# Delta-rule layers: v copied out by ScalarE, PSUM banks exchanged, output projection across the turn of a stage, VectorE's transpose and remainder later

## The chip, the cores and the metric

One core of a Trainium2 chip runs the whole program; its engines are TensorE, VectorE, ScalarE and GpSimd, and SyncE issues the DMAs. The metric is the device time of one execution in microseconds, here the median of three runs.

## The reference, cut to what matters

The program is a small audio tower: a convolutional token mixer, an attention and state-space layer, a mixture of experts, a fast-weight block and a second mixture of experts. The change touches the fast-weight block alone, which holds two delta-rule layers with a feed-forward part between them. One layer computes, for 16 sequences of 254 positions, 8 heads of 64:

```python
def step(W, inp):
    qt, kt, vt, bt = inp
    wk = jnp.einsum('bhde,bhe->bhd', W, kt)
    v_new = bt * (vt - wk)
    W = W + jnp.einsum('bhd,bhe->bhde', v_new, kt)
    out = jnp.einsum('bhde,bhe->bhd', W, qt)
    return (W, out)
...
h = layer_norm(x, ln_g, ln_b)
qkvb = jnp.einsum('sbi,oi->sbo', h, slow_w).reshape(slen, bsz, H, 3 * D + 1)
q, k, v, beta = jnp.split(qkvb, [D, 2 * D, 3 * D], axis=-1)
q = jax.nn.softmax(q, axis=-1)
k = jax.nn.softmax(k, axis=-1)
beta = jax.nn.sigmoid(beta)
attn = delta_rule(q, k, v, beta)
o = jnp.einsum('sbd,od->sbo', attn.reshape(slen, bsz, H * D), out_w)
return x + o
```

## The kernel before

`fast_weights` (L1487) handles one layer. A sequence of 254 positions is cut into two chunks of 127 (u = 0, 1). Within a chunk the recurrence is turned into a triangular system: A holds the products of keys with beta-scaled keys, its 32x32 diagonal blocks are inverted on VectorE, the blocks below the diagonal are joined by TensorE, and the system is solved against the right-hand side beta * v. The state goes from chunk 0 to chunk 1 through `next_state` and `carry`.

The layer is a software pipeline of 18 stages, written out by `stages` (L1590). In stage b each engine *prepares* batch b (projections, softmax, A, right-hand side, query-key products), *inverts* the diagonal blocks of batch b - 1, and *substitutes* (solves, outputs, output projection) batch b - 2. The first two stages and the last two do only some of this. Every engine has its own hand-written list of operations for a stage, and semaphores tie the lists together; nothing reorders them.

VectorE's list (from L2139): maximum and shift of the keys of both chunks, `turn_blocks` (L2107, the 32x32 transpose of the inverted blocks that came back by DMA), beta, sums and reciprocals, the queries' maxima and shifts, then the inversion of 31 steps, each a product (L2129) and a subtraction (L2133). Between its steps stand the queries' sums, `rest(0)` (L2098, the remainder for chunk 0, which needs TensorE's `join_rest`), the subtraction of the carried part (L2173), and `rest(1)`. After the inversion come the two right-hand sides (L2091), which read v in PSUM, `mask_qk(0)` (L2113), the addition of the output projection (L2184) and `mask_qk(1)`.

TensorE's list starts with the projections of keys, beta and queries (L1712), then `below_blocks` (L1768), the transposes of scaled keys and keys (L1723) with `corner_blocks` (L1784) between them, the first solve (L1800), `sum_a` (L1736), `join_rest` (L1813), the second solve (L1825), the v projection of chunk 0, `next_state`, `first_outputs`, `carry` (L1850), and so on; at the end stand `sum_qk(0)` (L1753), the output projection `project_out` (L1895) and `sum_qk(1)`, which waits for `rhs`, because v lies in the banks that it writes.

ScalarE takes the exponentials and copies results out of PSUM (L1954 transposes, L1961 A, L1968 the odd query-key products, L1975 solutions, L1981 corner blocks). GpSimd scales keys and queries (L1662, L1664, L1668), masks the odd query-key products (L1674) and resets `lane_x` (L1680). SyncE moves A and the inverse through DRAM.

The eight PSUM banks are shared by name. Keys are projected into banks 4 and 5, the same that `sum_qk(1)` fills and `mask_qk(1)` and `copy_qk(1)` read; queries go into 7 and 3, those of `sum_qk(0)`. So in the order above the keys' projection of the next stage waits for `mask_qk(1)`:

```python
PROJ_K, PROJ_Q, PROJ_V, BETA = (4, 5), (7, 3), (4, 5), 6
TURN_K, TURN_KB, TURN_Q = (4, 5), (6, 7), (3, 6)
SUM_A, SUM_QK = (4, 6), ((7, 3), (4, 5))
...
project("k", 0, PROJ_K[0], "qk_even", c)
project("k", 1, PROJ_K[1], "qk_copied", c)
```

## Time and profile before

| | us |
|---|---|
| median of 3 runs | 3041.76 (3034.02 to 3046.06) |
| the profiled execution | 3040.74 |
| its span, first to last instruction | 3039.0 |
| TensorE busy in the span | 2402.0 (79%) |
| VectorE busy | 2068.4 (68%) |
| ScalarE busy | 1234.0 (41%) |
| GpSimd busy | 747.4 (25%) |
| mean granted TensorE clock | 0.882 |

Busy shares are means over the whole program. The first delta-rule layer runs from about 1321 to 2006 us of the span, the second from about 2116 to 2810 us, the feed-forward part between them. In a timeline row stand start, duration, engine, line, operation, what it writes and reads, and in brackets the idle time before it with what ended that; PE is TensorE, DVE is VectorE, ACT is ScalarE, POOL is GpSimd. A TensorE row can hold many matmuls (x16). In a row of a stretch stand its ends and length, then the busy time (and instructions) of TensorE's matmuls and weight loads, VectorE, ScalarE and GpSimd, then the mean granted TensorE clock (1.00 is 2.4 GHz, 0.50 is 1.2 GHz), the DMA engines' share and GB/s. Matmuls are pipelined, so a busy TensorE is not one at its peak.

### The profile page before, as it was taken

What the parts mean: (1) busy time and instruction counts of PE and PEld (TensorE: products, weight loads), DVE (VectorE), ACT (ScalarE), POOL (GpSimd) and SP (SyncE); (2) the same over time, 40 slices, a digit from 0 to 9 for tenths busy, and PEclk for the clock granted to TensorE, in tenths of its full rate; (3) what the DMA queues carried; (4) which work ended last, traced back from release to release, by engine and by line L of the source; (5) the groups of instructions that cost most, each with busy time, mean ns of one, the idle gap of its engine ahead of it and who ended that gap; (6) DMA issues with size and microseconds to landing.
All of it is one profiled execution on the core that took longest, in us unless ns stands there. A gap on an engine that the chain in (4) does not pass through costs nothing. (4 is left out here: it accounts for less than half of the span.)

```text
span 3039.0 us, 44026 instructions
## 1 busy us (share of the span) xinstructions
PE 2402.0 (79%) x16426; PEld 1387.2 (46%) x16426; DVE 2068.4 (68%) x4427; ACT 1234.0 (41%) x1981; POOL 747.4 (25%) x712
## 2 busy tenths in 40 slices
PE   6747777778669999967888888687788888876598
PEld 2232222222234444335666666543466666665343
DVE  2256888888837777658888888613788888883332
ACT  3555555555432222343344443244334443431332
POOL 0005766676700000032222222101222222220000
PEclk9878998898879999988899999779789898986699
DMA  1000000000010000002222222100122222220000
GB/s 34 0 10 0 1 0 0 0 1 0 2 41 0 1 0 1 26 14 39 43 43 43 43 43 43 32 15 1 32 43 43 43 43 43 43 43 17 10 1 28
DMA packets 280818, 65.89 MB, mean 22 GB/s; under 512 B 272968, under 2 KB 274464, under 8 KB 280224
## 3 DMA queue, kind: packets, MB, share of 16 engines
q1 hardware_dynamic: 280608, 63.09, 11.2%
q8 instruction: 132, 2.16, 0.3%
q14 instruction: 78, 0.64, 0.1%
HBM read 44.20 MB, written 18.86 MB: 21 GB/s over the span
## 5 line engine op out<-in xcount | busy, mean ns | idle before, releaser
L949 POOL TENSOR_TENSOR ma_hc<-ma_state,ma_c 128x508 f32<-128x508 f32 x256 | 298.8, 1184 | 243.5 <-DVE ma_state L1048 144.3
L2133 DVE TENSOR_TENSOR fw_lane_x<-fw_lane_x,fw_lane_p 128x126 f32<-128x126 f32 (+22 forms) x992 | 326.8, 329 | 34.0
L2129 DVE TENSOR_TENSOR fw_lane_p<-fw_lane_a,fw_lane_x 128x126 f32<-128x126 f32 (+22 forms) x992 | 277.7, 280 | 29.6
L1712 PE MATMUL fw_p<-fw_w,fw_xs 128*127 128x512 f32 (+1 forms) x512 | 232.8, 589 | 54.0 <-DVE fw_qk L2113 26.3
L838 PE MATMUL ma_ps_y<-ma_hc,const 128*128 128x508 f32 x480 | 261.5, 672 | 16.4 <-POOL ma_hc L949 6.1
L1048 DVE TENSOR_TENSOR_SCAN ma_state<-ma_da,ma_ps_dbx 128x510 f32<-128x510 f32 x176 | 214.2, 1217 | 81.3 <-ACT ma_da L921 51.5
L1148 ACT ACTIVATE ex_sig<-ex_gate,ex_gate_scaled 128x508 f32<-128x508 f32 x128 | 87.6, 684 | 271.6 <-PE ex_gate L1118 271.6
L1674 POOL TENSOR_TENSOR fw_qk<-fw_qk,fw_masks 128x512 f32<-128x512 f32 x64 | 82.2, 1285 | 403.0 <-ACT fw_qk L1968 403.0
L838 PEld LDWEIGHTS ma_ps_y<-ma_hc,const 128*128 128x128 f32 x480 | 97.7, 213 | 154.3 <-issue 111.4
L1649 POOL MEMSET fw_k_rows<- 128x512 f32 x4 | 2.1, 525 | 659.1 <-POOLq L81 659.1
L1712 PEld LDWEIGHTS fw_p<-fw_w,fw_xs 128*127 128x127 f32 x512 | 91.4, 216 | 128.1 <-issue 118.8
L1975 ACT ACTIVATE fw_u_new<-fw_p 64x512 f32<-64x512 f32 x128 | 75.8, 592 | 159.5 <-PE fw_p L1825 107.6
L1109 PE MATMUL ex_total<-ex_weighted,ex_down 128*128 128x508 f32 x256 | 130.7, 592 | 10.8 <-DVE ex_weighted L1173 10.8
L1162 DVE SCALAR_TENSOR_TENSOR ex_gelu<-ex_gate,ex_bias,ex_sig 128x508 f32<-128x508 f32 x128 | 95.6, 747 | 64.0 <-ACT ex_sig L1148 64.0
L921 ACT ACTIVATE ma_da<-ma_dt,ma_a 128x508 f32<-128x508 f32 x176 | 124.2, 711 | 34.3 <-DVE ma_dt L995 34.2
L1668 POOL TENSOR_TENSOR fw_q_rows<-fw_q_rows,fw_total_q 127x512 f32<-127x512 f32 x64 | 66.8, 1043 | 285.9 <-DVE fw_total_q L2077 285.7
L1118 PE MATMUL ex_gate<-xn,ex_gate_up 128*128 128x508 f32 x256 | 131.7, 596 | 5.1 <-PEq L81 5.1
L1122 PE MATMUL ex_up<-xn,ex_gate_up 128*128 128x508 f32 x256 | 130.8, 593 | 0.0
L1753 PE MATMUL fw_p<-fw_q_t,fw_k_t 64*128 64x128 f32 x1024 | 75.7, 288 | 65.0 <-issue 65.0
L1042 DVE TENSOR_TENSOR ma_ps_dbx<-ma_ps_b,ma_dtx 128x508 f32<-128x508 f32 x176 | 118.5, 673 | 6.5 <-PE ma_ps_b L816 6.3
L1961 ACT ACTIVATE fw_a_t<-fw_p 128x1024 f32<-128x1024 f32 x64 | 65.6, 1024 | 114.3 <-PE fw_p L1813 95.2
L2302 DVE TENSOR_TENSOR ex_weighted<-ex_relu,ex_weight 128x508 f32<-128x508 f32 x64 | 43.8, 684 | 100.0 <-ACT ex_relu L2289 100.0
(310 smaller groups left out, 5149.4 us busy)
## 6 DMA issues: line engine op xcount, KB each, us to landing
fw_lane_a<-fw_a_dram SPq DMA_DIRECT2D x64, 256.0 KB, 4.2
fw_a_dram<-fw_a_t SPq DMA_DIRECT2D x128, 64.0 KB, 2.1
fw_x_dram<-fw_lane_x SPq DMA_DIRECT2D x64, 128.0 KB, 2.9
fw_x_rows<-fw_x_dram SPq DMA_DIRECT2D x128, 64.0 KB, 3.2
fw_x_t<-fw_x_dram SPq DMA_DIRECT2D x128, 64.0 KB, 2.7
x_in<-in_x SPq DMA_DIRECT2D x4, 512.0 KB
ex_gate_up<-in_gate_up SPq DMA_DIRECT2D x1, 2048.0 KB
out<-h SPq DMA_DIRECT2D x1, 2032.0 KB, 6.2
```

The lines of the kernel that those rows point to most:

```text
L838: pe.matmul(y_sum[h][:, 0:W2], k.ident, hc[(2 * n + h) % 8][:, :], start=n <= 1 and n - 1 in (-1, *PAIRED), stop=n == DS - 1)\
L921: act.activation(decay[:, :, 1:L + 1], two(dt[u][h][:, :]), ACT.Exp, scale=a[:, h, n:n + 1]).then_inc(s["da"], 1)
L949: pool.tensor_tensor(two(hc[m % 8][:, :]), state[m % 4][:, :, 1:L + 1], two(c_kept[n % 2][:, :]), ALU.mult).then_inc(s["hc"], 1)
L1042: dve.tensor_tensor(dbx[h][:, :, 1:L + 1], two(b_all[:, 0:W2]), two(dtx[u][h][:, :]), ALU.mult).then_inc(s["dbx"], 1)
L1048: dve.tensor_tensor_scan(line(state[m % 4][:, :, :]), line(decay), line(driven), 0.0, ALU.mult, ALU.add).then_inc(s["scan"], 1)
L1109: pe.matmul(total[:, 0:W2], down[:, e, j, :], weighted[n % 2][:, :], start=False, stop=n == NHF - 1).then_inc(s["downed"], 1)
L1118: pe.matmul(gate[j][:, 0:W2], gate_up[:, e, j * H:(j + 1) * H], x, start=True, stop=True).then_inc(s["gated"], 1)
L1122: pe.matmul(up[j][:, 0:W2], gate_up[:, e, I0 + j * H:I0 + (j + 1) * H], x, start=True, stop=True).then_inc(s["upped"], 1)
L1162: dve.scalar_tensor_tensor(gelu[j][:, :], gate[j][:, 0:W2], bias[:, e, j:j + 1], sig[j][:, :], ALU.add, ALU.mult).then_inc(s["gelu"], 1)
L1712: pe.matmul(bank[0:C, bk, u * NH:u * NH + n] if name == "beta" else bank[0:C, bk, 0:n], xs[:, u * C:(u + 1) * C], w[:, at:at + n], start=T ...
L2129: dve.tensor_tensor(p, lane_a[:, j:j + 1, j + 1:BLOCK].to_broadcast(shape), lane_x[:, 0:shape[1], j:j + 1].to_broadcast(shape), ALU.mult)\
L2133: dve.tensor_tensor(below, below, p, ALU.subtract).then_inc(inverted[j], 1)
```

## The change

- ScalarE copies v of each chunk from PSUM to a new tile `v_rows` (`copy_v`), the first behind `k_first`, the second behind `copy_a(1)`. The right-hand sides read this tile, and `sum_qk(1)` waits for the copy in place of `rhs`.
- Keys are projected and turned in banks 7 and 3, queries projected in 4 and 5. The keys' projection waits for `mask_qk(0)` and `copy_qk(0)` of the stage before, the queries' for `mask_qk(1)` and `copy_qk(1)`.
- `project_out` and the addition of its result are done a stage later: TensorE has them behind the queries' projections, VectorE behind the second `scale_kb`. A nineteenth stage holds only these two.
- On TensorE the first transpose of scaled keys stands ahead of `below_blocks`, and the second ones are exchanged.
- VectorE's `turn_blocks` moves from behind the keys' second shift to behind the queries' first, and `rest(0)` from behind step 8 of the inversion to behind step 10.

```diff
         q_rows = per("q_rows", [128, NH, D])
+        v_rows = per("v_rows", [C, NH, D])
...
-        PROJ_K, PROJ_Q, PROJ_V, BETA = (4, 5), (7, 3), (4, 5), 6
-        TURN_K, TURN_KB, TURN_Q = (4, 5), (6, 7), (3, 6)
+        PROJ_K, PROJ_Q, PROJ_V, BETA = (7, 3), (4, 5), (4, 5), 6
+        TURN_K, TURN_KB, TURN_Q = (7, 3), (6, 7), (3, 6)
...
                     if u == 0:
+                        pe.wait_ge(s["shift_q"], c + 2)
                         pe.wait_ge(s["k_t"], c + 2)
...
                         else:
-                            pe.wait_ge(s["rhs"], c + 2)
+                            pe.wait_ge(s["v"], c + 2)
...
                 def project_out():
-                    if not substitutes:
+
+                    if b < 3:
                         return
-                    pe.wait_ge(s["out_t"], upto[1])
+                    pe.wait_ge(s["out_t"], c - 4)
...
-                project("k", 0, PROJ_K[0], "qk_even", c)
-                project("k", 1, PROJ_K[1], "qk_copied", c)
+                project("k", 0, PROJ_K[0], "qk_even", max(c - 1, 0))
+                project("k", 1, PROJ_K[1], "qk_copied", max(c - 1, 0))
                 project("beta", 0, BETA, "q_t", c)
                 project("beta", 1, BETA, "q_t", c)
                 project("q", 0, PROJ_Q[0], "qk_even", c)
                 project("q", 1, PROJ_Q[1], "qk_copied", c)
+                project_out()
+                turn("kb", 0, kb[0], TURN_KB[0], "kb", "beta_exp", b + 1)
                 below_blocks()
-                turn("kb", 0, kb[0], TURN_KB[0], "kb", "beta_exp", b + 1)
                 turn("k", 0, k_rows[0], TURN_K[0], "rows_k", "shift_k", c + 1)
                 corner_blocks()
-                turn("kb", 1, kb[1], TURN_KB[1], "kb", "shift_q", c + 1)
                 turn("k", 1, k_rows[1], TURN_K[1], "rows_k", "shift_k", c + 2)
+                turn("kb", 1, kb[1], TURN_KB[1], "kb", "k_t", c + 1)
...
-                turn("q", 0, q_rows[0], TURN_Q[0], "rows_q", "shift_q", c + 2)
+                turn("q", 0, q_rows[0], TURN_Q[0], "rows_q", "k_t", c + 2)
...
                 sum_qk(0, 1)
-                project_out()
                 sum_qk(1, 0)
...
             stages(pe, stage)
+            stage(B + 2, 0, False, False, False)
...
+                def copy_v(u):
+                    if prepares:
+                        act.wait_ge(s["proj_v"], c + u + 1)
+                        act.wait_ge(s["rhs"], max(c + u - 1, 0))
+                        act.activation(v_rows[u][:, :, :], heads(bank[0:C, PROJ_V[u], :]), ACT.Copy)\
+                            .then_inc(s["v"], 1)
...
                     act.wait_ge(s["proj_beta"], c + 2)
+                    act.wait_ge(s["rhs"], c)
...
+                copy_v(0)
                 solved(1, 0)
                 copy_a(1)
+                copy_v(1)
                 turned("q", 0, TURN_Q[0], q_t[par][0])
...
-                        dve.wait_ge(s["proj_v"], c + u + 1)
+                        dve.wait_ge(s["v"], c + u + 1)
...
-                        dve.tensor_tensor(rhs[par][u][0:C], heads(bank[0:C, PROJ_V[u], :]), wide(beta[:, u]), ALU.mult)\
+                        dve.tensor_tensor(rhs[par][u][0:C], v_rows[u][:, :, :], wide(beta[:, u]), ALU.mult)\
...
+                def add_outputs():
+
+                    if b >= 3:
+                        r_at = k.r[:, cols(b - 3, L)]
+                        dve.wait_ge(s["projected"], b - 2)
+                        dve.tensor_tensor(r_at, bank[:, PROJECT, 0:L], r_at, ALU.add).then_inc(s["added"], 1)
...
                 shift("k", 1)
-                turn_blocks()
...
                 maximum("q", 0)
                 shift("q", 0)
+                turn_blocks()
                 sums("k", 1)
                 inverse_sums("k", 1)
                 scale_kb(1)
+                add_outputs()
                 maximum("q", 1)
                 shift("q", 1)
                 go_on(0, 6)
                 sums("q", 0)
                 inverse_sums("q", 0)
-                go_on(6, 8)
+                go_on(6, 10)
                 rest(0)
-                go_on(8, 12)
+                go_on(10, 12)
...
                 mask_qk(0)
-                if substitutes:
-                    r_at = k.r[:, cols(b - 2, L)]
-                    dve.wait_ge(s["projected"], batches)
-                    dve.tensor_tensor(r_at, bank[:, PROJECT, 0:L], r_at, ALU.add).then_inc(s["added"], 1)
                 mask_qk(1)

             stages(dve, stage)
+            stage(B + 2, 0, False, False, False)
```

## Rows read from the trace of the kernel before

**Rows 1.** Busy time by stretch: steady part of the first delta-rule layer.

```profile
1379.00:1892.00 513.00, 425.28 (x5409) 326.20 (x5408) 433.07 (x1183) 208.37 (x351) 126.56 (x129) 0.90 0.25 41
```

**Rows 2.** Waits of VectorE in that stretch: us in total, times, longest us.

```profile
DVE fw_top_k L2056 <- PE fw_p L1712: 20.8, 16, 2.2
DVE fw_rhs L2098 <- PE fw_p L1813: 12.2, 10, 2.1
```

**Rows 3.** Timeline of VectorE (start us, us, ..., [idle before]): first and last steady stage.

```profile
1379.08 0.69 DVE L2056 TENSOR_REDUCE fw_top_k<-fw_p 127x8 f32<-127x512 f32 x1 [2.23 <-PE fw_p L1712]
...
1892.31 0.69 DVE L2056 TENSOR_REDUCE fw_top_k<-fw_p 127x8 f32<-127x512 f32 x1 [1.28 <-PE fw_p L1712]
```

**Rows 4.** Timeline of VectorE in the reference stage.

```profile
1695.61 0.69 DVE L2056 TENSOR_REDUCE fw_top_k<-fw_p 127x8 f32<-127x512 f32 x1 [1.28 <-PE fw_p L1712]
...
1699.07 0.71 DVE L2107 STREAM_TRANSPOSE fw_x_turned<-fw_x_rows 128x512 f32<-128x512 f32 x1 [0.71 <-DMA fw_x_rows<-fw_x_dram]
...
1704.61 0.93 DVE L2129 TENSOR_TENSOR fw_lane_p<-fw_lane_a,fw_lane_x 128x31 f32<-128x31 f32 x1
...
1711.81 0.69 DVE L2098 TENSOR_TENSOR fw_rhs<-fw_rhs,fw_p 64x512 f32<-64x512 f32 x1 [0.82 <-PE fw_p L1813]
1712.53 0.28 DVE L2129 TENSOR_TENSOR fw_lane_p<-fw_lane_a,fw_lane_x 128x115 f32<-128x115 f32 x1
...
1717.81 0.69 DVE L2173 TENSOR_TENSOR fw_rhs<-fw_rhs,fw_p 128x512 f32<-128x512 f32 x1
...
1728.68 0.19 DVE L2129 TENSOR_TENSOR fw_lane_p<-fw_lane_a,fw_lane_x 128x16 f32<-128x16 f32 x1
1728.91 1.14 DVE L2133 TENSOR_TENSOR fw_lane_x<-fw_lane_x,fw_lane_p 128x16 f32<-128x16 f32 x1
1730.08 1.29 DVE L2091 TENSOR_TENSOR fw_rhs<-fw_p,fw_beta 127x512 f32<-127x512 f32 x2
1731.29 0.68 DVE L2113 TENSOR_TENSOR fw_qk<-fw_p,fw_masks 128x512 f32<-128x512 f32 x1
...
1732.67 0.69 DVE L2113 TENSOR_TENSOR fw_qk<-fw_p,fw_masks 128x512 f32<-128x512 f32 x1 [0.37 <-PE fw_p L1753]
1734.64 0.69 DVE L2056 TENSOR_REDUCE fw_top_k<-fw_p 127x8 f32<-127x512 f32 x1 [1.28 <-PE fw_p L1712]
```

**Rows 5.** Timeline of GpSimd in the reference stage.

```profile
1704.44 1.04 POOL L1664 TENSOR_TENSOR fw_k_rows<-fw_k_rows,fw_total_k 127x512 f32<-127x512 f32 x1
...
1728.69 1.32 POOL L1674 TENSOR_TENSOR fw_qk<-fw_qk,fw_masks 128x512 f32<-128x512 f32 x1 [9.72 <-ACT fw_qk L1968]
1733.34 1.27 POOL L1674 TENSOR_TENSOR fw_qk<-fw_qk,fw_masks 128x512 f32<-128x512 f32 x1 [3.34 <-ACT fw_qk L1968]
```

**Rows 6.** Timeline of TensorE in the reference stage.

```profile
1694.48 4.11 PE L1712 MATMUL fw_p<-fw_w,fw_xs 128*127 128x512 f32 x12 [0.88 <-DVE fw_qk L2113]
...
1716.23 1.11 PE L1850 MATMUL fw_p<-fw_state,fw_kb_t 64*128 64x64 f32 x16
...
1727.89 1.99 PE L1895 MATMUL fw_p<-fw_out_t,fw_w_out 128*128 128x254 f32 x8
1731.47 1.16 PE L1753 MATMUL fw_p<-fw_q_t,fw_k_t 64*128 64x128 f32 x16 [1.59 <-issue]
```

**Rows 7.** Timeline of ScalarE in the reference stage.

```profile
1724.86 0.59 ACT L1975 ACTIVATE fw_u_new<-fw_p 64x512 f32<-64x512 f32 x1 [1.33 <-PE fw_p L1825]
...
1728.01 0.60 ACT L1968 ACTIVATE fw_qk<-fw_p 128x512 f32<-128x512 f32 x1
```

**Rows 8.** A turn at the low clock: timelines, then two stretches.

```profile
1578.51 0.69 DVE L2056 TENSOR_REDUCE fw_top_k<-fw_p 127x8 f32<-127x512 f32 x1 [2.23 <-PE fw_p L1712]
...
1576.43 6.21 PE L1712 MATMUL fw_p<-fw_w,fw_xs 128*127 128x512 f32 x10 [0.88 <-DVE fw_qk L2113]
...
1576.43:1582.64 6.21, 6.21 (x11) 3.17 (x12) 3.77 (x7) 1.44 (x3) 1.66 (x2) 0.52 0.98 160
...
1578.51:1616.32 37.81, 31.70 (x417) 23.48 (x417) 33.32 (x91) 15.90 (x27) 9.29 (x10) 0.95 0.25 38
```

More of the change, by code:

```diff
@@ L1579, in fast_weights @@
             "exp_k", "exp_q", "total_k", "total_q", "recip_k", "recip_q", "rows_k", "rows_q",
-            "beta_exp", "beta_one", "beta", "kb", "rhs", "k_first", "turn_k", "turn_q", "turn_kb", "k_t", "q_t",
+            "beta_exp", "beta_one", "beta", "kb", "v", "rhs", "k_first", "turn_k", "turn_q", "turn_kb", "k_t", "q_t",
             "kb_t", "a_sum", "a_t", "qk_sum", "qk_even", "qk_copied", "qk_odd",
```

## The prediction

> **What bounds the kernel now.** Start with the busy times by stretch. In the steady part of the first delta-rule layer VectorE is busy 433 of 513 us and TensorE 425 [rows 1]. TensorE's figure also counts small matmuls that wait on others; VectorE's order of work is what the waits speak of. The waits of VectorE in that stretch are the second view: 20.8 us ahead of the keys' maximum (L2056) for TensorE's projection and 12.2 us ahead of the remainder (L2098) for TensorE's join [rows 2]. The third is VectorE's timeline. Thirteen stages take 1892.31 - 1379.08 = 513.2 us, 39.5 us each [rows 3]. Each layer has 14 stages that do all three parts (batches 2 to 15), so 28 in all; the second layer runs the same code and I count its stages alike.
>
> As reference I take one stage, from the keys' maximum at 1695.61 to the next at 1734.64: T = 1695.61, length 39.03 us [rows 4]. VectorE waits there 0.71 us (transpose L2107, for a DMA), 0.82 us (remainder), 0.37 us (second mask) and 1.28 us (the next keys). It also loses time that no wait shows: the last operation of the inversion takes 1.14 us, though the one before it, of the same 128x16 elements, takes 0.19 us [rows 4]; GpSimd's mask runs from 1728.69 to 1730.01 [rows 5]. The first product of the inversion takes 0.93 us in the same way, while GpSimd scales k_rows from 1704.44 to 1705.48 [rows 4, 5]. So a VectorE operation with both inputs in SBUF stands still while GpSimd works, and ends about 0.05 us behind it.
>
> **The change part by part,** on the reference stage.
>
> *Up to the subtraction of the carried part (L2173),* now at T + 22.20. Moving the transpose behind the first queries' shift takes away its 0.71 us wait: it would start some 5.1 us after T, while the data landed 3.46 us after T. GpSimd's second scaling then starts 0.71 us earlier, but the added output (L2184, 0.41 us) now stands ahead of the inversion, so the first product is held some 0.4 us less. VectorE would come to the remainder at T + 16.20 - 0.71 - 0.82 - 0.41 + 0.41 + 1.24 = T + 15.91, where 1.24 us are the two inversion steps that now precede it, each of two operations of 0.28 us (the row at 1712.53) with 0.03 us behind them [rows 4]. TensorE delivered its part just before T + 16.20 in this stage, so the two meet within a few tenths, and I take no wait. From the remainder's end to the end of the carry, TensorE and ScalarE need 1717.34 - 1712.50 = 4.84 us [rows 4, 6]; nothing in that chain is touched. So the carry ends at T + 15.91 + 0.69 + 4.84 = T + 21.44, and the subtraction starts at about T + 21.48. VectorE itself would be there at 22.20 - 0.71 - 0.82 - 0.41 + 0.41 = T + 20.67 and waits 0.8 us: this is what comes late next, and the 1.24 us put ahead of the remainder pay for it. **Gain 0.72 us.** Bounds: nothing, if TensorE comes later to the remainder; 1.5 us, if the subtraction need not wait.
>
> *From there to the end of the inversion* nothing moves: 12.24 us, the hold of 0.95 us (1.14 - 0.19) in it.
>
> *The right-hand side* (L2091, two operations, 1.29 us) reads v from SBUF instead of PSUM. ScalarE's two copies have the shape of its 0.60 us copy at 1728.01; they lie in its idle time, 1.33 us ahead of 1724.86 for one [rows 7]. Without that cover they would cost 0.6 us each. The price lies elsewhere: both inputs of L2091 are now in SBUF. And the wait of the second query-key products for `rhs` is gone, so they need not start at 1731.47; their other wait, for the queries' copy, is over when ScalarE goes on to the next copy at 1728.01 [rows 6, 7]. From there: 0.1 + 1.16 us of products, 0.6 us of copy, so GpSimd's second mask is ready at about 1729.97, where its first ends (1730.01) and the right-hand side begins (1730.08). Now it runs at 1733.34, beside work that reads PSUM [rows 5]. One of the three operations there would be held for the mask's 1.27 us, less the 0.15 us by which a held one overlaps its tail: **cost 1.1 us.** Bounds: 0, if both operations go ahead of the mask, and 1.3, the mask's whole length. I take 1.1, the value nearest the two held rows, in both of which GpSimd got in between VectorE's operations. The Trainium skill (SBUF — State Buffer, Who interferes with whom) says that whichever of the two starts first holds the shared ports for its whole instruction and the other blocks fully. The held rows agree with it. By that rule the order of arrival at 1730 us decides, and with VectorE's pair first the sum would be lower by this term.
>
> *The turn.* Now the first mask ends at 1731.97, and then come the added output, the 0.37 us wait, the second mask and 1.28 us for the projection: 2.67 us to the next keys. With the banks exchanged the projection needs only the first mask: 1.28 us after it, with the second mask (0.69 us) inside. **Gain 1.39 us.**
>
> *TensorE's clock at the turn.* Where TensorE runs at 1.2 GHz there, the wait for the keys is 2.23 us instead of 1.28; the six projections take 6.21 us instead of 4.11, at a mean granted clock of 0.52 [rows 6, 8]. The wait is longer than 1.6 us at 10 of the 28 turns into such stages now (one of them is shown), and what precedes it is little work on TensorE. Now its idle time there is 1.59 us, 1.16 us of products, then 0.88 us [rows 6]. After the change the output projection (1.99 us) is gone from this place, the products end at about 1729.3, and the projection starts at 1731.97 + 1.1 + 0.12 = 1733.2: one idle stretch of 3.9 us. So I take the low clock at nearly all turns: **cost 0.8 us** of the 0.95, because some falls will come behind the first projection. Bounds 0 and 0.95. What the low clock delays behind the turn I leave out: the stage that follows the low turn shown took 37.81 us at a mean clock of 0.95, shorter than the reference [rows 8].
>
> *Covered or neutral.* The output projection now lies between the query projections and the transposes, where TensorE waits anyhow for the turned blocks (at full clock it ends at 1698.59 + 1.99, which is T + 4.97, and they come at T + 5.1 + 0.71 [rows 4, 6]); without that cover it costs up to 1.99 us. The new waits of ScalarE's beta and of the k transposes are for things done a few us before. In the filling stages the copy adds 0.7 us ahead of the right-hand side and the exchanged banks save as much; in the draining ones the same projection and addition stand in a nineteenth stage, behind the same wait for `out_t`. All these I cost at 0, within 2 us a layer.
>
> **Sum.** 39.03 - 0.72 + 1.1 - 1.39 + 0.8 = 38.8 us a stage, against the mean of 39.5: 28 x 0.7 = 20 us. The profiled execution took 3040.74 us (span 3039.0), which gives 3021; the median of the runs shown is 1.0 higher, so I predict **3022 us**.
>
> **The rivals.**
> *The right-hand side goes first.* Both of its operations follow without a gap, GpSimd waits for them, and the masks read PSUM and pass. Then the 1.1 us fall away: 37.7 us a stage, 28 x 1.8 = 50 us, 2991. For it: the two sit back to back (1.29 us for two of 0.69). Against it: GpSimd entered between inversion operations every time it is seen.
> *The gain comes back as a later wait.* With transpose, output projection and turned blocks all later on TensorE, the join could come 1.5 us after VectorE's arrival, and the subtraction with it; then what is saved early is waited for at L2098 and L2173: 39.5 us a stage, 3042. For it: 12.2 us of such waits stand already [rows 2], and the transpose moves back by about 1.7 us from T. Against it: the remainder itself moves back by 1.24 us, which leaves TensorE almost as much time as it loses.
> *Slower: the low clock lasts through the output projection.* It falls in the idle stretch, the six projections take 2.1 us more, and the output projection, now ahead of the transposes, at the same ratio 3.0 us or more instead of 1.99. The blocks below the diagonal then start about 4 us after their place now (T + 8.4 instead of T + 4.3), the join comes 2 us after VectorE, and a stage takes 38.97 + 2.0 = 41.0 us, 1.5 more than now. From half of the stages on, this eats the gain; in three of four it gives 28 x (0.75 x 1.5 - 0.25 x 0.6) = +27 us, 3068. For it: the longer idle stretch, and the six projections of rows 8, all at the low clock. Against it: the stage behind them, at 0.95.
>
> **How the numbers follow.** Chances: forecast 0.50, right-hand side first 0.22, gain waited for later 0.14, slower 0.14. The forecast's own range, from its bounds, is 3006 to 3036. A measurement here can tell about 0.5%, 15 us: faster means below 3027, slower above 3057. Of the forecast some 0.35 lies below 3027 and 0.15 within; with the first rival faster is 0.57, same 0.29, slower 0.14. The range 2983 to 3050 takes in most of the first rival and all of the second, and leaves out the greater part of the slower case and the end of the first.
>
> **What would show it.** In the new profile: no wait ahead of L2107's transpose; a wait of about 0.8 us ahead of the carried subtraction; one of the right-hand side's operations, or the last inversion one, at 1.7 to 1.8 us (or 1.3) next to GpSimd's second mask; the granted clock near half over the projections; the wait ahead of the keys' maximum between 1.3 and 2.3 us less the second mask's 0.6. It is wrong if the right-hand side takes 0.69 us each with the mask behind it, or if the wait ahead of the remainder grows past 1.5 us.

## The result, and the profile after

The kernel after takes 3051.01 us (median of 20 runs, 3040.29 to 3066.80), the kernel before 3041.41 us in the same series (20 runs, 3033.35 to 3048.66). The ratio is 1.0034, with a 95% interval of 1.0022 to 1.0046: slower, by 10 us or 0.3%, and outside the range of the prediction, just above its upper end of 3050. The profiled execution took 3051.16 us (span 3049.3), so that the trace speaks for the median.

The thirteen stages of the first layer come first, as a row of a stretch, then VectorE's waits in them (us in total, times, longest us).

```profile
1380.10:1898.40 518.30, 419.79 (x5401) 314.64 (x5401) 442.52 (x1182) 217.89 (x377) 132.55 (x131) 0.91 0.25 42
```

```profile
DVE fw_top_k L2070 <- PE fw_p L1713: 23.4, 25, 1.6
DVE fw_rhs L2195 <- PE fw_p L1852: 19.1, 13, 2.5
DVE fw_rhs L2112 <- PE fw_p L1815: 0.4, 2, 0.2
```

A stage takes 518.3 / 13 = 39.9 us, 0.4 more than before [rows 1, 3]. The wait ahead of the remainder, 12.2 us before [rows 2], has shrunk to 0.4 (it is L2112 now), as was meant. In its place stand 19.1 us ahead of the subtraction of the carried part (L2195), where the waits of before show one of 1.2 us:

```profile
DVE fw_rhs L2173 <- PE fw_p L1850: 1.2, 1, 1.2
```

The wait for the keys (L2070) has not shrunk: 23.4 us for 20.8.

VectorE's timeline shows where in a stage that is. The first two rows belong to one stage, T = 1699.02, the others to the next, T = 1739.73, up to the keys of the one behind it.

```profile
1715.24 0.69 DVE L2112 TENSOR_TENSOR fw_rhs<-fw_rhs,fw_p 64x512 f32<-64x512 f32 x1
...
1722.42 0.69 DVE L2195 TENSOR_TENSOR fw_rhs<-fw_rhs,fw_p 128x512 f32<-128x512 f32 x1 [2.45 <-PE fw_p L1852]
...
1739.73 0.69 DVE L2070 TENSOR_REDUCE fw_top_k<-fw_p 127x8 f32<-127x512 f32 x1 [1.41 <-PE fw_p L1713]
...
1741.44 0.69 DVE L2070 TENSOR_REDUCE fw_top_k<-fw_p 127x8 f32<-127x512 f32 x1 [0.29 <-PE fw_p L1713]
...
1745.28 0.70 DVE L2121 STREAM_TRANSPOSE fw_x_turned<-fw_x_rows 128x512 f32<-128x512 f32 x1
...
1748.62 0.60 DVE L2150 TENSOR_TENSOR fw_lane_p<-fw_lane_a,fw_lane_x 128x31 f32<-128x31 f32 x1
...
1755.94 0.69 DVE L2112 TENSOR_TENSOR fw_rhs<-fw_rhs,fw_p 64x512 f32<-64x512 f32 x1
...
1761.53 0.69 DVE L2195 TENSOR_TENSOR fw_rhs<-fw_rhs,fw_p 128x512 f32<-128x512 f32 x1 [0.85 <-PE fw_p L1852]
...
1772.62 1.23 DVE L2154 TENSOR_TENSOR fw_lane_x<-fw_lane_x,fw_lane_p 128x16 f32<-128x16 f32 x1
1773.77 2.35 DVE L2105 TENSOR_TENSOR fw_rhs<-fw_v_rows,fw_beta 127x512 f32<-127x512 f32 x2
1776.15 1.29 DVE L2127 TENSOR_TENSOR fw_qk<-fw_p,fw_masks 128x512 f32<-128x512 f32 x2
1779.07 0.69 DVE L2070 TENSOR_REDUCE fw_top_k<-fw_p 127x8 f32<-127x512 f32 x1 [1.63 <-PE fw_p L1713]
```

Against the reference stage [rows 4] the transpose no longer waits, and the first product of the inversion takes 0.60 us for 0.93. The right-hand sides take 2.35 us for 1.29; beside them stands GpSimd's row, where the masks of both chunks follow each other (before, 3.3 us apart [rows 5]):

```profile
1772.54 3.03 POOL L1675 TENSOR_TENSOR fw_qk<-fw_qk,fw_masks 128x512 f32<-128x512 f32 x2 [9.52 <-ACT fw_qk L1979]
```

The new wait of 0.85 or 2.45 us is explained on TensorE: the second solve behind the remainder in the reference stage of before, then, in the same two stages of after, that solve, the carry, and the turn.

```profile
1712.64 1.12 PE L1825 MATMUL fw_p<-fw_rhs,fw_x_t 128*64 128x64 f32 x16 [0.87 <-DVE fw_rhs L2098]
```

```profile
1716.08 1.12 PE L1827 MATMUL fw_p<-fw_rhs,fw_x_t 128*64 128x64 f32 x16 [2.48 <-DVE fw_rhs L2112]
...
1721.26 1.11 PE L1852 MATMUL fw_p<-fw_state,fw_kb_t 64*128 64x64 f32 x16
...
1756.78 1.12 PE L1827 MATMUL fw_p<-fw_rhs,fw_x_t 128*64 128x64 f32 x16 [2.48 <-DVE fw_rhs L2112]
...
1760.37 1.11 PE L1852 MATMUL fw_p<-fw_state,fw_kb_t 64*128 64x64 f32 x16
...
1776.99 6.83 PE L1713 MATMUL fw_p<-fw_w,fw_xs 128*127 128x512 f32 x12 [3.83 <-DVE fw_qk L2127]
```

TensorE stands 2.48 us in both stages, waiting for VectorE's remainder, where in the reference stage it stood 0.87 us ahead of the same solve. The wait has changed sides. From the start of that solve to the end of the carry TensorE then needs 6.29 us in one stage and 4.70 in the other. The granted clock of the stretches from the remainder to the subtraction tells them apart (the third stretch is the turn ahead of T = 1739.73; columns as in [rows 1]):

```profile
1715.20:1722.40 7.20, 6.33 (x67) 4.80 (x67) 4.47 (x12) 1.57 (x3) 1.04 (x1) 0.76 0.01 3
1755.90:1761.50 5.60, 4.72 (x67) 3.69 (x67) 4.47 (x12) 1.57 (x3) 1.04 (x1) 1.00 0.01 3
1736.70:1741.40 4.70, 3.53 (x6) 1.51 (x6) 2.98 (x5) 0.22 (x1) 0.61 (x1) 0.65 1.12 195
```

The timelines and clocks of all 26 steady stages, 13 in each layer, fall into three kinds. In 10 TensorE stands 2.48 us, goes at 1.2 GHz for part of this chain (granted clock 0.76), and VectorE waits 2.45 us. In 8 it stands the same 2.48 us, goes at 2.4 GHz (1.00), and VectorE waits 0.85. In the other 8 the clock is low further up, from T + 3 to the join (0.84 or 0.85); TensorE then stands only 0.88 or 1.20 us, the chain goes at 1.00, and VectorE waits 0.85. The order of the kinds is the same in both layers. (Two of the expectations below say 9 for the first kind; it is 10, five in each layer.) At every turn between these stages the clock is low (0.50 to 0.57 over the projections), behind an idle stretch of 3.83 us.

Why TensorE now stands so long is seen ahead of the join. One group of transposes and the stretch from T + 3 to the end of the join, first in the reference stage of before, then in the stage T = 1739.73 of after:

```profile
1706.07 1.11 PE L1723 MATMUL fw_p<-const,fw_kb 128*128 128x128 f32 x4
...
1698.61:1711.76 13.15, 10.63 (x192) 9.21 (x192) 11.09 (x31) 6.41 (x11) 5.13 (x5) 0.74 0.08 13
```

```profile
1750.33 0.66 PE L1724 MATMUL fw_p<-const,fw_kb 128*128 128x128 f32 x4
...
1742.73:1754.30 11.57, 10.64 (x203) 8.54 (x201) 10.78 (x32) 6.28 (x11) 5.13 (x5) 1.00 0.07 11
```

In the reference stage the clock was low in part of this stretch, and the join ended at T + 16.15. In the stage of after the whole stretch goes at 2.4 GHz and the join ends at T + 14.57, though the output projection now stands ahead of it. In the kernel before 21 of the 26 stages have 0.63 to 0.72 from T + 3 on; in the kernel after 18 have 1.00. So TensorE comes earlier to the remainder, while VectorE comes to it later (T + 16.16 on the means, for T + 15.38).

The means over these 26 stages, from T, put the two kernels side by side (us; from the timelines of both traces):

| | before | after |
|---|---|---|
| start of the remainder (wait before it) | 16.34 (0.96) | 16.22 (0.06) |
| start of the carried subtraction (wait before it) | 22.44 (0.12) | 22.42 (1.47) |
| end of the inversion | 34.71 | 34.74 |
| end of the right-hand sides | 36.03 | 37.01 |
| end of VectorE's first mask | 36.62 | 37.73 |
| next keys | 39.54 | 39.87 |

### The profile page after: what moved, and what is told of

It reads as the page before. It is cut to its first block and busy times, and to the rows that moved or that the text cites. A ratio compares the mean times of both kernels' runs of the same rounds, so it can differ in the third digit from the quotient of the medians.

```text
span 3049.3 us, 44218 instructions
## 1 busy us (share of the span) xinstructions
PE 2393.6 (78%) x16426; PEld 1368.2 (45%) x16426; DVE 2089.8 (69%) x4427; ACT 1258.6 (41%) x2045; POOL 757.9 (25%) x712
## 5 line engine op out<-in xcount | busy, mean ns | idle before, releaser
L1713 PE MATMUL fw_p<-fw_w,fw_xs 128*127 128x512 f32 (+1 forms) x512 | 275.0, 679 | 147.3 <-DVE fw_qk L2127 119.7
L2150 DVE TENSOR_TENSOR fw_lane_p<-fw_lane_a,fw_lane_x 128x126 f32<-128x126 f32 (+22 forms) x992 | 267.5, 270 | 29.6
L1713 PEld LDWEIGHTS fw_p<-fw_w,fw_xs 128*127 128x127 f32 x512 | 106.2, 247 | 244.7 <-issue 235.0
L1675 POOL TENSOR_TENSOR fw_qk<-fw_qk,fw_masks 128x512 f32<-128x512 f32 x64 | 93.2, 1458 | 286.0 <-ACT fw_qk L1979 284.2
L1949 ACT ACTIVATE fw_k_rows<-fw_k_rows 127x512 f32<-127x512 f32 x64 | 40.3, 630 | 247.6 <-DVE fw_k_rows L2079 247.6
L1827 PE MATMUL fw_p<-fw_rhs,fw_x_t 128*64 128x64 f32 x1024 | 78.0, 234 | 61.1 <-DVE fw_rhs L2112 61.1
L1663 POOL TENSOR_TENSOR fw_kb<-fw_k_rows,fw_kb_scale 127x512 f32<-127x512 f32 x64 | 66.8, 1043 | 188.6 <-DVE fw_kb_scale L2097 188.6
```

Of the source, the lines that this page charges most:

```text
L1713: pe.matmul(bank[0:C, bk, u * NH:u * NH + n] if name == "beta" else bank[0:C, bk, 0:n], xs[:, u * C:(u + 1) * C], w[:, at:at + n], start=T ...
L2150: dve.tensor_tensor(p, lane_a[:, j:j + 1, j + 1:BLOCK].to_broadcast(shape), lane_x[:, 0:shape[1], j:j + 1].to_broadcast(shape), ALU.mult)\
```

## The experiments

The theory: a remainder that comes late leaves TensorE idle, its clock falls in the idle stretches there and at the turn, and GpSimd's mask holds the right-hand side. The main rival: the chain from the remainder to the subtraction is late at full clock too, or it is the new order at the turn that costs. Sixteen kernels were run beside the one of the change; "ratio" is against the kernel before, with its 95% interval. The exchange of the banks, the output projection's new place and the later transpose were not run each by itself; what is said of them is read from rows.

**The remainder back behind step 8** (kernel after, nothing else):

```diff
-                go_on(6, 10)
+                go_on(6, 8)
                 rest(0)
-                go_on(10, 12)
+                go_on(8, 12)
```

> The changed kernel with the remainder back behind step 8 of the inversion. Theory (the late remainder leaves TensorE idle ahead of its second solve, its clock falls in 9 of 26 stages, and the carry is late): the remainder starts near T + 15.0 instead of T + 16.2, the wait ahead of the carried subtraction shrinks from 0.85 or 2.45 us to below 0.5 us in all stages, the subtraction starts at T + 20.7 to 21.0 instead of 22.4 on the mean, a stage takes 38.2 to 38.7 us instead of 39.87, the time is about 3012 us. Rival (TensorE's own chain sets the carry, wherever the remainder stands): the subtraction stays at T + 21.8 or later, 3045 to 3055 us.

Measured: 3033.83 us, ratio 0.9967 (0.9949 to 0.9985). The wait ahead of the carried subtraction is 0.03 us in every stage, as the theory has it. But the stages alternate between 38.35 and 40.15 us, because in every second one the remainder is waited for, 1.8 us (waits of VectorE, from 1380 to 1893 us):

```profile
DVE fw_top_k L2070 <- PE fw_p L1713: 24.2, 25, 1.6
DVE fw_rhs L2112 <- PE fw_p L1815: 11.6, 7, 1.8
```

So 17 us come back by undoing this move alone, less than half of the 39 expected; the rest goes to a fall of the clock ahead of the join, which the theory had not priced (granted clock 0.82 from T + 3 on in the slower stages, 1.00 in the others).

**The converse: the late remainder alone, in the kernel before**

```diff
-                go_on(6, 8)
+                go_on(6, 10)
                 rest(0)
-                go_on(8, 12)
+                go_on(10, 12)
```

> The kernel before with one part of the change alone: the remainder of chunk 0 stands behind step 10 of the inversion in place of step 8. Nothing is left out. Theory (TensorE's clock falls in the stretch between its join and the carry because it waits there for a late remainder, wherever the rest of the work stands): VectorE comes to the remainder 15.38 + 1.24 = 16.6 us behind the keys' maximum, TensorE delivered at 16.34 on the mean, so the wait there goes from 0.96 to 0.1 us or less; the carry is ready 5.57 us behind the remainder's start, at 22.2, and VectorE waits about 0.8 us for it at full clock; in a quarter to a half of the stages it waits 2.4 us with a granted clock of 0.5 between join and carry. Stage 39.6 to 40.0 us, time 3043 to 3055. Rival (the falls there come from the other order at the turn and the output projection's new place): a wait of 0.8 us ahead of the carried subtraction in every stage and no fall there, stage 39.2 to 39.3, time 3032 to 3037.

Measured: 3047.24 us, ratio 1.0027 (1.0009 to 1.0045). The stage has 39.68 us; the remainder's wait is gone (0.04), and 0.85 us ahead of the carried subtraction stand in 22 of 26 stages, 2.4 to 3.4 in four:

```profile
DVE fw_rhs L2173 <- PE fw_p L1850: 19.2, 13, 3.4
```

The move pays for its own gain at full clock and loses where the clock falls. The time lies where the theory put it, but the low clock comes in fewer stages (4 of 26) than the quarter to half that it named.

**Idle stretches filled.** Matmuls of 512 columns, whose result nobody reads, keep TensorE busy; they add work and leave nothing out. In the kernel after, first at the turn, then between the join and the second solve of chunk 0, then in both places:

```diff
                 join_rest(0)
+                if substitutes and prepares:
+                    for n in range(2):
+                        pe.matmul(bank[:, OUT, 0:512], k.ident, w[:, 0:512], start=True, stop=True)
...
                 sum_qk(1, 1)
+                if substitutes and prepares:
+                    pe.wait_ge(s["out_t"], upto[1])
+                    for n in range(3):
+                        pe.matmul(bank[:, OUT, 0:512], k.ident, w[:, 0:512], start=True, stop=True)
```

> The changed kernel with three extra 128x512 matmuls behind the second query-key products, into a bank that is rewritten before anyone reads it; they do no work of the reference. Theory (the idle stretch of 3.9 us on TensorE brings its clock to 1.2 GHz for the next projections, which costs the keys' maximum 0.7 to 0.9 us): the granted clock stays at 1.0 over the turn, the wait ahead of the keys' maximum falls from 1.4 to 1.63 us to about 0.7 us, about 3027 us. Rival (the extra matmuls stand ahead of the projection and delay it, or the clock falls anyway): the wait stays or grows, 3051 us or more.

Measured: 3025.64 us, ratio 0.9938 (0.9913 to 0.9962). The keys are waited for 0.68 us in every stage behind a filled turn, and the wait ahead of the second keys' maximum is gone. The waits ahead of the carried subtraction remain (1.44 us on the mean).

> The changed kernel with two extra 128x512 matmuls between TensorE's join and its second solve, into a bank that is rewritten before anyone reads it; they do no work of the reference. Theory (the wait for the late remainder lets TensorE's clock fall, which makes the carry late in 9 of 26 stages): no stage has the clock at 0.5 from T + 18.6 on, the wait ahead of the carried subtraction is about 0.85 us in all stages, 28 x 0.5 us less, about 3036 us. Rival (the clock falls for another reason, or the chain is as long at full clock): waits of 2.45 us remain, 3048 to 3055 us.

Measured: 3043.17 us, ratio 1.0000 (0.9983 to 1.0016). Between the remainder and the subtraction the clock is 1.00 in all 26 stages, as the theory has it. But the time expected was 3036, and half of the gain is missing: 18 stages wait 0.85 us for the carry, 8 wait 1.5 to 1.85, and in these the clock is low ahead of the join (0.81 to 0.85), so that the extra matmuls stand in the way of the solve. The stage takes 39.61 us. Part of the falls only moved.

> The kernel after with two matmuls of 512 columns between the join and the second solve of chunk 0 and three behind the last query-key products; their result is not used, nothing is left out. Theory (what the step up to the carried subtraction missed is TensorE's clock alone): the wait for the keys is 0.68 us, that ahead of the second keys' maximum is gone, the wait ahead of the carried subtraction is 0.85 in every stage: 39.34 - 0.73 - 0.29 = 38.3 us a stage, time 3051 - 28 x (39.87 - 38.3) = 3007, bounds 3000 to 3015. Rival (the clock falls in another stretch then, or the chain from remainder to carry is late at full clock too): 38.7 us or more a stage, 3018 to 3030, as with the fill at the turn alone.

Measured: 3005.60 us, ratio 0.9870 (0.9839 to 0.9902), and 38.31 us a stage. The stretch of thirteen stages and its waits:

```profile
1377.70:1874.30 496.60, 448.11 (x5531) 320.59 (x5531) 441.53 (x1182) 216.76 (x377) 132.68 (x131) 0.99 0.25 43
```

```profile
DVE fw_rhs L2202 <- PE fw_p L1852: 13.1, 13, 1.5
DVE fw_top_k L2077 <- PE fw_p L1713: 10.1, 14, 1.6
```

At a mean granted clock of 0.99 the subtraction starts at T + 21.41 or T + 21.42 in most stages (predicted: 21.48) and the kernel is 45 us faster than after, although TensorE does more. The theory's number was 3007. In 7 stages of the 26 VectorE waits 1.5 us and in one 1.85, where the theory had 0.85 in every one. The rival, a chain that is late at full clock too, falls: at full clock the wait is 0.85, near the 0.8 of the prediction.

**GpSimd's masks made to wait.** A wait in GpSimd's loop keeps its mask behind the right-hand sides, first for the second mask alone:

```diff
                 for u in chunks:
+                    if u == 1:
+                        pool.wait_ge(s["rhs"], c + 2)
                     pool.wait_ge(s["qk_copied"], c + u + 1)
```

> The changed kernel with one wait more: GpSimd's second query-key mask waits until both right-hand sides are done. Theory (the right-hand side is held by that mask because both its inputs lie in SBUF): the two right-hand sides take 1.3 us instead of 2.35, the next keys come about 1.0 us earlier, 28 x 1.0 us less, about 3023 us. Rival (the right-hand side is slower by itself, from its source or its broadcast factor): it stays near 2.3 us and the time at 3051 us or above.

Measured: 3003.96 us, ratio 0.9873 (0.9845 to 0.9901). The right-hand sides take 1.28 us again (VectorE's timeline; the operation ahead of them is still held, by the first mask):

```profile
1714.56 1.23 DVE L2156 TENSOR_TENSOR fw_lane_x<-fw_lane_x,fw_lane_p 128x16 f32<-128x16 f32 x1
1715.71 1.28 DVE L2107 TENSOR_TENSOR fw_rhs<-fw_v_rows,fw_beta 127x512 f32<-127x512 f32 x2
```

This shows the hold; the rival, a right-hand side that is slower by itself, falls. The gain is 1.6 us a stage and not the 1.0 expected, because the turn's idle stretch on TensorE shrinks too, from 3.83 to 2.76 us: the keys are then waited for 0.68 us in 19 of 26 stages.

**VectorE's first mask ahead of the right-hand sides**, so that the keys' projection starts earlier (kernel after):

```diff
+                mask_qk(0)
                 right_hand_side(0)
                 right_hand_side(1)
-                mask_qk(0)
                 mask_qk(1)
```

> The changed kernel with VectorE's first query-key mask ahead of the two right-hand sides. Theory (of the turn's 5.1 us from the end of the inversion to the next keys, the hold by GpSimd's mask and the projection's wait are the cost, and the mask of 0.7 us is all that the projection needs): the first mask runs beside GpSimd's, a right-hand side is held about 0.5 us instead of 1.07, the projection runs beside the right-hand sides at full clock and the keys' maximum waits for nothing; 3.0 to 3.2 us from the inversion's end to the next keys, a stage of 37.9 us or less, 2990 us or less. Rival (the clock at the turn falls for the idle time that is left, and the right-hand sides are held in full): a stage of 39 us, 3025 to 3051.

Measured: 3000.47 us, ratio 0.9867 (0.9834 to 0.9899); from the end of the inversion to the next keys 3.0 us, as expected. The time was expected at 2990 or less and missed that by 10 us: the clock now falls at the start of the stage (0.65 to 0.75 from T + 3 on in 20 of 26 stages), and waits ahead of the remainder (0.60 us on the mean) and the subtraction (1.17) stay. With the remainder back behind step 8 as well:

> Both the first mask ahead of the right-hand sides and the remainder behind step 8. Theory: the gains add, a stage of 37.0 us or less in most stages, 2975 us or less. Rival (TensorE's clock falls ahead of the join instead and the remainder waits 1.8 us in every second stage, as it did with the earlier remainder alone): no better than with the mask first alone.

Measured: 3005.03 us, ratio 0.9868 (0.9836 to 0.9901). The wait moved from the subtraction to the remainder, 1.77 us on the mean: the rival. Where the clock falls ahead of the join, the remainder's place was worth nothing here.

**The copy of v.** The kernel after without the copies:

```diff
-                            pe.wait_ge(s["v"], c + 2)
+                            pe.wait_ge(s["rhs"], c + 2)
...
-                copy_v(0)
...
-                copy_v(1)
...
-                        dve.wait_ge(s["v"], c + u + 1)
+                        dve.wait_ge(s["proj_v"], c + u + 1)
...
-                        dve.tensor_tensor(rhs[par][u][0:C], v_rows[u][:, :, :], wide(beta[:, u]), ALU.mult)\
+                        dve.tensor_tensor(rhs[par][u][0:C], heads(bank[0:C, PROJ_V[u], :]), wide(beta[:, u]), ALU.mult)\
```

> The changed kernel without the copy of v: the right-hand sides read PSUM again and the second query-key products wait for them; banks, output projection, transpose and remainder stay as changed. Theory (with the banks exchanged the copy brings no wait to an end that matters, and its price is the hold): the right-hand sides take 1.3 us, the second products fill TensorE's idle stretch, the next keys come 3.7 to 4.2 us after the inversion instead of 5.1, a stage of 38.6 us or so, about 3015 us. Rival (the copy is needed, for the second products now delay the projection of the next keys and the mask behind it): 5 us or more from the inversion to the next keys, 3045 us or more.

Measured: 3044.85 us, ratio 1.0005 (0.9990 to 1.0020). The right-hand sides take 1.29 us, but VectorE's second mask then waits 0.7 to 1.62 us for its products, and from the end of the inversion to the next keys it is some 4.8 us, for 5.1 in the kernel after. The expectation of 3015 missed and the time is the rival's: the copy's hold costs about what the copy saves elsewhere. The comparison is not clean, since the clock falls in the chain in 15 stages here and in 10 in the kernel after. The kernel before with the copies alone (the same lines the other way round, with `copy_v` as in the change; banks, order and output projection as before):

> The kernel before with another part alone: v is copied out by ScalarE, the right-hand sides read the copy, and the second query-key products wait for the copy in place of the right-hand sides; banks, order and output projection stay as before. Nothing is left out. Theory (two operands in SBUF let GpSimd's second mask in between, as in the kernel after): the pair of right-hand sides takes 2.3 to 2.4 us in place of 1.29, the wait ahead of VectorE's second mask (0.37 us) is gone, the wait for the next keys stays 1.3 to 2.2 us, since they are still projected behind that mask. From the end of the inversion to the next keys 5.3 to 5.6 us in place of 4.8, time 3055 to 3065. Rival (the second products, copied and masked earlier, give back what the hold takes): 4.8 us or less, time 3035 to 3045.

Measured: 3039.74 us, ratio 1.0001 (0.9971 to 1.0030). The expectation missed, the hold does not come. Rows of VectorE, GpSimd and TensorE at the end of one stage:

```profile
1731.25 1.28 DVE L2101 TENSOR_TENSOR fw_rhs<-fw_v_rows,fw_beta 127x512 f32<-127x512 f32 x2
...
1732.97 1.27 POOL L1675 TENSOR_TENSOR fw_qk<-fw_qk,fw_masks 128x512 f32<-128x512 f32 x1 [1.69 <-ACT fw_qk L1976]
...
1729.18 1.98 PE L1896 MATMUL fw_p<-fw_out_t,fw_w_out 128*128 128x254 f32 x8
1731.09 1.16 PE L1754 MATMUL fw_p<-fw_q_t,fw_k_t 64*128 64x128 f32 x16
```

Here the output projection still stands ahead of the second products, GpSimd's mask becomes ready only at 1732.97, and the right-hand sides, with the same two operands in SBUF, run through. So the copy alone does not bring the hold; by these rows it also takes second products that are ready earlier, with the output projection out of their way. No run moved the projection alone. The Trainium skill (SBUF — State Buffer, Who interferes with whom) says that the order of issue, not the form of the operation, decides who blocks. The 1.28 us here and 2.35 us in the kernel after, for the same statement, agree with it.

**Put together.** Remainder behind step 8 and the second mask waiting:

> The changed kernel with GpSimd's second mask behind the right-hand sides and the remainder back behind step 8. Theory (the two losses are of different places, so their gains add: 1.6 us a stage from the mask's wait, 0.6 us from the earlier remainder, as measured one by one): 37.6 us a stage, 2986 us. Rival (both gains come from the same falls of TensorE's clock, which go elsewhere): no better than the mask's wait alone, 3004 us.

Measured: 2975.02 us, ratio 0.9774 (0.9747 to 0.9801), 37.22 us a stage. Expected were 2986. The two gain more than their sum: the remainder is waited for 0.35 us on the mean, where it was 0.89 with the early remainder alone, and the subtraction 0.09, where it was 1.64 with the mask alone. That each shortens a stretch in which the clock fell for the other fits these waits but is not shown. Then both masks waiting:

```diff
                 for u in chunks:
-                    if u == 1:
-                        pool.wait_ge(s["rhs"], c + 2)
+                    pool.wait_ge(s["rhs"], c + 2)
                     pool.wait_ge(s["qk_copied"], c + u + 1)
```

> The kernel after with the remainder back behind step 8 of the inversion and both of GpSimd's masks (not the second alone) waiting for the second right-hand side. Nothing is left out. Theory (the last operation of the inversion, 1.14 us where the one before it takes 0.19, is held by the first mask in the same way): it takes 0.2 us, the right-hand sides stay at 1.2 us for the pair, the stage loses another 0.9 us against the version in which the second mask alone waits: 2975 - 28 x 0.9 = 2950, bounds 2945 to 2960. Rival (the hold moves to the next operation with both operands in SBUF, or the wait for the next keys takes it up, since it is TensorE's projection behind the first mask that ends last): 2970 to 2980.

Measured: **2932.84 us, ratio 0.9640** (0.9617 to 0.9663), 35.64 us a stage. VectorE's timeline and GpSimd's:

```profile
1729.52 0.19 DVE L2155 TENSOR_TENSOR fw_lane_x<-fw_lane_x,fw_lane_p 128x16 f32<-128x16 f32 x1
1729.62 1.28 DVE L2106 TENSOR_TENSOR fw_rhs<-fw_v_rows,fw_beta 127x512 f32<-127x512 f32 x2
...
1730.99 2.49 POOL L1676 TENSOR_TENSOR fw_qk<-fw_qk,fw_masks 128x512 f32<-128x512 f32 x2 [11.41 <-DVE fw_rhs L2106]
```

The last operation of the inversion takes 0.19 us for 1.23, and no operation is held in its place. The gain was expected at 25 us and is 42: beside the 0.96 us that the operation loses, the mean granted clock of the thirteen stages is 0.98 where it was 0.95 (0.91 in the kernel after). The same wait in the kernel before:

> The kernel before with one change alone: both of GpSimd's masks wait for the second right-hand side. Nothing is left out. Theory (only the hold of the last inversion operation goes, since the right-hand side reads PSUM there): that operation takes 0.2 us in place of 1.14, the stage 38.6 in place of 39.5, time 3041 - 27 = 3015, bounds 3005 to 3022. Rival (the gain of the version with both masks waiting rests on the holds alone, so that most of its 108 us come here too): below 2990. Other rival (the clock takes it up at the turn): 3030 to 3040.

Measured: 3014.96 us, ratio 0.9910 (0.9881 to 0.9939), as the theory of the hold alone has it (3015): 38.66 us a stage, 0.88 less. And with the remainder where the change puts it:

> The kernel after with both of GpSimd's masks waiting for the second right-hand side, and the remainder where the kernel after has it, behind step 10 of the inversion; nothing is left out. Against the version with the remainder behind step 8 this differs in the remainder's place alone. Theory (a late remainder costs its wait at full clock, and a fall of TensorE's clock in some stages): 0.85 us ahead of the carried subtraction in most stages, 2.4 in a few, stage 36.5 to 36.9 in place of 35.6, time 2933 + 28 x 0.9 to 1.3 = 2957 to 2968. Rival (without the holds the turn keeps TensorE awake, and the remainder's place costs nothing): 2930 to 2940.

Measured: 2978.55 us, ratio 0.9776 (0.9742 to 0.9809). The two kernels differ in the remainder's place alone, and by 46 us. The waits, here and then in the faster one:

```profile
DVE fw_rhs L2196 <- PE fw_p L1853: 28.4, 13, 2.5
DVE fw_top_k L2071 <- PE fw_p L1714: 9.8, 13, 1.6
```

```profile
DVE fw_top_k L2071 <- PE fw_p L1714: 13.5, 18, 1.6
DVE fw_rhs L2113 <- PE fw_p L1816: 2.3, 2, 1.3
```

With the late remainder the carried subtraction waits 2.4 us in 22 of 26 stages, though the turn is now at full clock nearly everywhere; with the early one a single stage waits for it, 1.2 us. This is the clearest evidence that the late remainder brings the fall. Its price was not foreseen: 2957 to 2968 were expected, with 2.4 us in a few stages only. At last the filled turn on top of the two early versions:

> The kernel after with the remainder back behind step 8, GpSimd's second mask waiting for the second right-hand side, and three matmuls of 512 columns, whose result is not used, behind the last query-key products; nothing is left out. Theory (the keys' wait of 0.68 to 1.63 us, 1.17 on the mean, is TensorE's clock at the turn): it is 0.68 in every stage, and the 0.3 us ahead of the second keys' maximum go too; 28 x 0.5 to 0.8 us off 2975: 2953 to 2961. Rival (the fall of the clock moves on to the start of the next stage and delays the join): waits of 1.2 to 1.8 us ahead of the remainder in most stages, 2975 to 2990.

Measured: 2964.51 us, ratio 0.9748 (0.9719 to 0.9777). The gain is 10 us where 14 to 22 were expected: the keys wait 0.68 us in every stage, but in 8 of 26 the remainder is waited for, about 1 us, as the rival has it.

> The kernel after with the remainder behind step 8, both of GpSimd's masks waiting for the second right-hand side, and three matmuls of 512 columns, whose result is not used, behind the last query-key products; nothing is left out. Theory: the wait for the keys, 0.68 to 1.63 us there, is 0.68 in every stage, and the 0.3 us ahead of the second keys' maximum go: stage 35.2 in place of 35.6, time 2933 - 12 = 2921, bounds 2915 to 2928. Rival (the turn is short enough by now, the fill only brings a fall elsewhere): 2930 to 2945.

Measured: 2945.70 us, ratio 0.9675 (0.9643 to 0.9708): slower than without the fill, where the theory had 2921; the time is at the upper end of the rival. The turn is short by now, the three matmuls stand in the projection's way, and the keys are waited for 1.36 us at a granted clock of 1.00 (0.91 us on the mean without the fill). That is the larger part of the 0.54 us that a stage loses; the rest is waits ahead of the remainder and the subtraction.

## Why the prediction was wrong, by its own steps

**Up to the subtraction of the carried part: this step failed.** It put the subtraction at T + 21.48 for T + 22.20 in the reference stage, a gain of 0.72 us. On the means it came at 22.42 for 22.44: a gain of 0.02. The 0.70 us that did not come are 20 us over 28 stages. Its lower bound, nothing, was reached, but not for the reason given there, a late TensorE. Against T + 21.48 the subtraction came 0.94 us later: 0.62 from falls of the clock in the chain, 0.26 from behind the turn, 0.06 from small waits and shifts. (0.24 us of the 0.94 belong to the base, below: the reference stage was at 22.20 where the mean was at 22.44.) Three sentences of the step failed.

- "Nothing in that chain is touched" took the chain's 4.84 us from a stage in which TensorE had waited 0.87 us ahead of it. With a remainder that VectorE brings late, TensorE stood 2.48 us in 18 of 26 stages, and in 10 of them its clock fell in the chain, 1.6 us each or 0.62 us on the mean.
- "What the low clock delays behind the turn I leave out" put at nothing what cost 0.29 us ahead of the second keys' maximum in most stages (0.26 on the mean).
- "The two meet within a few tenths" priced a later remainder by VectorE's own path. TensorE was ready at 1756.78 - 2.48 = 1754.30 in the second stage shown, and VectorE came at 1755.94: the late party was VectorE. The step took TensorE's delivery, just before T + 16.20, from a stage with the low clock ahead of the join (0.74), and took the low clock at the turn beside it. The stage of the low turn that the prediction itself shows, T = 1578.51, has both together: 0.96 from T + 3 on, the join done at T + 13.96, and TensorE standing 1.85 us ahead of the solve.

```profile
1594.32 1.12 PE L1825 MATMUL fw_p<-fw_rhs,fw_x_t 128*64 128x64 f32 x16 [1.85 <-DVE fw_rhs L2098]
```

That the chain holds at full clock is shown by the version with both stretches filled: T + 21.4. That the late remainder brings the fall is shown by the pair of 46 us. Why the clock falls behind a wait of 2.48 us in 10 stages and not behind the same wait in 8 others is not settled; undoing one part moved the fall to the join or to the turn.

**The base of the sum: this failed too.** The gain of 0.7 us a stage hid a choice: the terms themselves sum to 0.2 us, and the other 0.5 was the distance of the reference stage (39.03) from the mean (39.5), with the low clock of other stages in it, some 13 us over 28 stages that no edit makes. With the 20 us above this is more than the 29 us by which 3051 missed 3022; the right-hand sides give part of it back, since they cost 0.95 us a stage on the means (2.27 us from the end of the inversion to their end, for 1.32) and not 1.1.

**To the end of the inversion:** 12.24 us predicted, 12.32 measured.

**The right-hand side:** right in place and size. Cost 1.1 predicted; the pair takes 1.06 us more in the stage shown, and its end stands 0.98 us later on the means. The rival in which it goes first is out. It goes first where the copy is made and the output projection stays in its place.

**The turn and its clock:** right together. From the first mask's end to the next keys 2.67 - 1.39 + 0.8 = 2.08 us were to be left; it is 39.87 - 37.73 = 2.14 on the means. The one idle stretch was put at 3.9 us and is 3.83, and the low clock, put at nearly all turns, is there at all between the steady stages.

**Covered or neutral:** right for the output projection, since the remainder does not wait. In the filling stages of the first layer the first is 3 us longer (24.34 for 21.39) and the second 1.4 shorter, within the 2 us a layer.

**The rivals:** the later wait came, in the place that the second rival names, but not by its cause: it had TensorE late. The slower rival, with a join that comes late behind a low clock that lasts, did not: the wait ahead of the remainder is 0.06 us on the mean.

## What to carry to other kernels

When a wait of one engine is removed by giving it other work first, look who waits then: a wait that goes over to TensorE can cost more than its own length, because the clock of the chain behind it may fall, so price that chain at both clocks. Ask of every mask or scaling on GpSimd beside VectorE operations with two inputs in SBUF in which order they become ready; a wait that keeps GpSimd behind them cost nothing here and gave 28 us in the old kernel (3042.99 to 3014.96) and, with the remainder early, 101 us in the new one (3033.83 to 2932.84). Take the mean of the stages as the base of a sum, not a quiet one, and take no engine's timing from a stage whose clock is not the one that is forecast.

## What was not expected of the hardware

Five matmuls a stage whose result nobody reads made the program 45 us faster, and the granted clock of the stretch went from 0.91 to 0.99. The Trainium skill (TensorE: Matmul & The Clock Gate, HAM oscillation — how this bites in real kernels) tells of a kernel that pays for the fall of the clock anew in every round of waiting. Here the ten stages with a wait of 2.45 us, one of them shown at 0.76 between remainder and subtraction, are such rounds; eight others, with the same wait of TensorE, pay nothing in that chain.

Gains were not additive: the second mask's wait gave 47 us, the early remainder 17, both 76. And a fall could seldom be removed by one edit: it moved between turn, join and carry.
